# One chain for the RMS norm and the query layer norm, its scale folded into Wq, in a gated cross-attention kernel on Trainium2

## What is computed

```python
# layer 0
memory_proj = ctx @ W_mem.T
attn = softmax(x @ memory_proj.T / sqrt(256))
memory_context = attn @ memory_proj
gate = sigmoid(concat([x, memory_context]) @ W_gate.T + b_gate)
fused = x + gate * memory_context
x = fused * rsqrt(mean(fused ** 2) + 1e-6) * norm_w
# layer 1, 16 heads of 64
qn = (x - mean(x)) * rsqrt(var(x) + 1e-5) * ln_q_g + ln_q_b
q = qn @ Wq * 64 ** -0.5
k, v = split(ctx @ Wkv)
attn = softmax(where(mask, q @ k.T, lowest))
x = x + tanh(attn_gate) * ((attn @ v) @ Wo)
h = layernorm(x) * ln_ff_g + ln_ff_b
x = x + tanh(ff_gate) * (gelu(h @ W1) @ W2)
```

## Time and profile before

| | |
|---|---|
| median of 3 runs | 231.49 us (231.4 to 231.99) |
| profiled execution, its own time | 232.58 us |
| its span | 230.7 us |
| busy share PE, DVE, ACT, POOL | 92%, 61%, 55%, 34% |
| mean granted TensorE clock | 0.993 |

### The profile page before, as it was taken

How to read it: one execution, slowest core, us unless ns; L and a number is a source line. 1 busy time by engine, 2 the same in 40 slices (tenths; PEclk the granted TensorE clock), 3 DMA queues, 4 the chain that set the end, 5 groups by cost and what they waited for, 6 DMA issues and landing times.

```text
span 230.7 us, 4263 instructions
## 1 busy us (share of the span) xinstructions
PE 212.7 (92%) x1520; PEld 170.0 (74%) x1520; DVE 141.8 (61%) x296; ACT 127.4 (55%) x414; POOL 79.5 (34%) x82
## 2 busy tenths in 40 slices
PE   7769997998999999999999977999989999999994
PEld 4546544766976978976989855778867788998993
DVE  1575997635885556985655887867875567125410
ACT  3365754747457646567636466575449775028600
POOL 2030143943175333266331447636373007000000
PEclk9999997999999999999999999999999999999999
DMA  6984005050000000000000000050000000110011
GB/s 203 351 300 149 0 0 182 3 185 0 0 3 0 3 1 1 3 1 0 3 0 4 0 0 0 3 182 0 3 1 3 1 0 4 47 45 0 4 47 53
DMA packets 8463, 10.30 MB, mean 45 GB/s; under 512 B 754, under 2 KB 7668, under 8 KB 8052
## 3 DMA queue, kind: packets, MB, share of 16 engines
q1 hardware_dynamic: 7908, 9.71, 12.3%
q10 hardware_dynamic: 528, 0.26, 0.4%
HBM read 8.92 MB, written 1.05 MB: 43 GB/s over the span
## 4 chain that ended last, share of the span: by engine, by line
PE 56%; issue 13%; DVE 11%; POOL 10%; ACT 9%; POOLq 0%; ACTq 0%; DVEq 0%
PE bank L379 33%; ACT expd L585 6%; POOL probs L481 5%; PE bank L1080 4%; PE bank L1171 4%; PE bank L1050 3%; PE bank L1027 3%; PE bank L1090 3%; DVE neg_max L784 2%; PE bank L1229 2%; POOL wo_pair L519 1%; DVE probsT L797 1%; PE bank L1116 1%; PE bank L1134 1%; PE bank L1126 1%
## 5 line engine op out<-in xcount | busy, mean ns | idle before, releaser
L585 ACT ACTIVATE expd<-bank,neg_max 128x128 f32<-128x128 f32 (+1 forms) x136 | 50.5, 396 | 38.1 <-DVE neg_max L784 38.0
L481 POOL TENSOR_TENSOR probs<-expd,row_rcp 128x512 f32<-128x512 f32 x40 | 42.3, 1069 | 69.8 <-DVE row_rcp L792 63.2
L784 DVE TENSOR_REDUCE neg_max<-bank 128x4 f32<-128x512 f32 (+1 forms) x40 | 25.7, 683 | 6.0 <-PE bank L1050 3.6
L585 ACT ACTIVATION_READ_ACCUMULATOR expd<-bank,neg_max 128x1 f32 x136 | 29.3, 216 | 0.0
L379 PE MATMUL bank<-xhT_pair,wq_pair 128*128 128x256 f32 x192 | 27.5, 293 | 1.1 <-DVE fused L806 1.1
L379 PEld LDWEIGHTS bank<-xhT_pair,wq_pair 128*128 128x128 f32 x192 | 24.6, 194 | 5.0 <-DVE fused L806 1.9
L379 PE MATMUL bank<-wo_pair,oT_pair 128*128 128x256 f32 x192 | 26.6, 288 | 0.0
L1080 PE MATMUL bank<-ident,probs 128*128 128x128 f32 x160 | 22.6, 277 | 3.7 <-POOL probs L481 3.5
L379 PEld LDWEIGHTS bank<-wo_pair,oT_pair 128*128 128x128 f32 x192 | 23.6, 189 | 1.8
L1080 PEld LDWEIGHTS bank<-ident,probs 128*128 128x128 f32 x160 | 17.7, 140 | 8.4 <-POOL probs L481 7.1
L379 PE MATMUL bank<-wq_pair,gelu_pair 128*128 128x256 f32 x192 | 23.2, 281 | 0.4 <-issue 0.3
(11 more groups left out here) (125 smaller groups left out, 346.9 us busy)
## 6 DMA issues: line engine op xcount, KB each, us to landing
stage<-in_L_xattn_W_dram SPq DMA_DIRECT2D x2, 1024.0 KB, 5.0
x_sb<-in_x_dram SPq DMA_DIRECT2D x4, 256.0 KB, 8.7
wkv_sb<-in_L_xattn_Wkv_dram SPq DMA_DIRECT2D x1, 1024.0 KB, 9.2
stage<-in_L_xattn_Wq_dram SPq DMA_DIRECT2D x1, 1024.0 KB, 10.3
stage<-in_L_xattn_Wo_dram SPq DMA_DIRECT2D x1, 1024.0 KB, 5.4
...
```

Source lines behind the costliest of these rows:

```text
L481: nc.gpsimd.tensor_tensor(probs[:, r, :].rearrange("p (h k) -> p h k", h=hb), expd[:, r, :].rearrange("p (h k) -> p h k", h=hb), row_rcp[: ...
L585: last = nc.scalar.activation(expd[:, r, h * w:(h + 1) * w], SC[n % 2][:, h * w:(h + 1) * w], ACT.Exp, bias=neg_max[:, r, h:h + 1], accum_ ...
L784: nc.vector.tensor_reduce(neg_max[:, r, 0:hb], SC[n % 2][:, :].rearrange("p (h k) -> p h k", h=hb), AX_X, ALU.max, negate=True).then_inc(d ...
```

## The change

The two norms become one chain. DVE no longer waits for the root mean square: it multiplies `fused` by `norm_w` alone, takes the statistics of that product, and works out both quantities whose roots are needed (`squares`); POOL takes the four roots at once. `xhat` scales by the second root, since the RMS factor cancels in a layer norm, apart from the epsilon, which is corrected. POOL multiplies `x_sb` by the first root afterwards, for the residual. The stages `x1` and `ln1` are gone; `rms` now does on DVE what they did, in the place of `rms`.

`ln_q_g` is folded into Wq as a scale per partition, and `ln_q_b` into a bias `q_bias`, which 16 matmuls with one moving column make in the prologue (`qbias`) and which DVE adds where it copied `q` before. So POOL's two passes over `xhat` are gone, and `xhT` waits for DVE.

Key banks are copied out whole, the odd ones by ACT and the even ones by DVE. The prologue is put in another order. The loads of `ln_q_g` and `ln_q_b` are 128x2 elements now and stand right behind Wq.

```diff
-    ("k", "hot", 0), ("splitq", 0), ("k", "hot", 3), ("gate", 0), ("k", "hot", 1), ("fuse", 0), ("rms", 0),
-    ("k", "hot", 2), ("k", "hot", 4), ("xT", 1), ("x1", 0), ("ln1", 0), ("k", "hot", 6), ("xhat", 0), ("k", "hot", 5),
-    ("y", 1), ("splitq", 1), ("k", "hot", 7), ("scores", "ctx", 1, 0), ("v", "hot", 0, 0), ("flag",), ("tiles",),
-    ("v", "hot", 1, 0), ("xhT", 0), ("v", "hot", 0, 1), ("norm", "ctx", 1, 0), ("exp", "ctx", 1, 0), ("q", 0, 0),
-    ("splito", 0), ("splito", 1), ("v", "hot", 1, 1),
+    ("k", "hot", 0), ("splitq", 0), ("k", "hot", 1), ("gate", 0), ("qbias",), ("k", "hot", 2), ("fuse", 0), ("rms", 0),
+    ("splitq", 1), ("k", "hot", 3), ("k", "hot", 4), ("xT", 1), ("xhat", 0), ("k", "hot", 5), ("tiles",),
+    ("y", 1), ("k", "hot", 6), ("xhT", 0), ("flag",), ("k", "hot", 7), ("scores", "ctx", 1, 0), ("q", 0, 0),
+    ("v", "hot", 0, 0), ("exp", "ctx", 1, 0), ("v", "hot", 0, 1), ("norm", "ctx", 1, 0),
+    ("splito", 0), ("splito", 1), ("v", "hot", 1, 0), ("v", "hot", 1, 1),
...
-    ((("x1", 1),), (("ln1", 1), ("q", 0, 3), ("xT", 2)), (("xhat", 1),)),
+    ((("xhat", 1),), (("q", 0, 3), ("xT", 2)), ()),
...
+                            gp.wait_ge(pool["x1"], c - 1)
+                        nc.gpsimd.tensor_tensor(roots[:, :, :].rearrange("p a t -> p (a t)"),
+                                                squares[:, :, :].rearrange("p a t -> p (a t)"), half_pow[:, :], ALU.pow
                                                 ).then_inc(pool["rstd"], 1)
...
+                        rows = x_sb[:, st[1] * T:(st[1] + 1) * T, :]
+                        gp.wait_ge(dve["xhat"], c)
+                        gp.wait_ge(pool["rstd"], c)
+                        nc.gpsimd.tensor_tensor(
+                            rows, rows, rms_r.rearrange("p (t a) -> p t a", a=1).to_broadcast([P, T, D]),
+                            ALU.mult).then_inc(pool["x1"], 1)
...
                     elif kind == "rms":
-                        ve_.wait_ge(act["square"], c)
-                        nc.vector.tensor_scalar(ms[:, :], sumsq[:, :], 1.0 / D, RMS_EPS, ALU.mult, ALU.add
-                                                ).then_inc(dve["ms"], 1)
-                    elif kind == "x1":
 
                         b = st[1]
-                        ve_.wait_ge(pool["rms"], c)
                         if c == 1:
                             ve_.wait_ge(w_in["normw"], 16)
+                        ve_.wait_ge(dve["gated"], T * c)
                         for t in range(T):
-                            last = nc.vector.scalar_tensor_tensor(
-                                x_sb[:, b * T + t, :], fused[:, t, :], rms_r[:, t:t + 1], normw_sb[:, :],
-                                ALU.mult, ALU.mult)
+                            last = nc.vector.tensor_tensor(x_sb[:, b * T + t, :], fused[:, t, :], normw_sb[:, :],
+                                                           ALU.mult)
                         chain(last)
                         tile_stats(b)
-                    elif kind == "ln1":
                         aggregate(mean_var, 0)
-                        nc.vector.tensor_scalar(ve[:, :], mean_var[:, :, 1], LN_EPS, None, ALU.add
-                                                ).then_inc(dve["ve"], 1)
+                        ve_.wait_ge(act["square"], c)
+                        if c > 1:
+                            ve_.wait_ge(pool["rstd"], c - 1)
+                        chain(nc.vector.tensor_scalar(ms, sumsq[:, :], 1.0 / D, RMS_EPS, ALU.mult, ALU.add))
+                        nc.vector.scalar_tensor_tensor(ve, ms, LN_EPS, mean_var[:, :, 1], ALU.mult, ALU.add
+                                                       ).then_inc(dve["ve"], 1)
...
+                        for pair in range(PAIRS):
+                            for k in range(K):
+                                last = nc.tensor.matmul(
+                                    path.bank(st)[:, pair:pair + 1], stage[:, k * INNER + pair * P:k * INNER + (pair + 1) * P],
+                                    lnq_cols[:, 1, k:k + 1], start=k == 0, stop=k == K - 1)
+                        last.then_inc(pe["qbias"], 1)
                     elif kind in ("xhT", "h2T"):
-                        te.wait_ge(pool["affine"], c if kind == "xhT" else B + c)
+                        if kind == "xhT":
+                            te.wait_ge(dve["xhat"], c)
```

More of the change, by code:

```diff
@@ L221, in gated_attention_block @@
         sumsq = sb("sumsq", [P, T])
-        ms = sb("ms", [P, T])
-        rms_r = sb("rms_r", [P, T])
-        ve = sb("ve", [P, T])
-        rstd = sb("rstd", [P, T])
+        squares = sb("squares", [P, 2, T])
+        ms, ve = squares[:, 0, :], squares[:, 1, :]
+        roots = sb("roots", [P, 2, T])
+        rms_r, rstd = roots[:, 0, :], roots[:, 1, :]
         ve2 = sb("ve2", [P, B, T])
@@ L280, in gated_attention_block @@
         out_done = sem("out_done")
-        pe = {k: sem(f"pe_{k}") for k in ("xT", "ctxT", "gatew", "gatem", "mask", "y", "scores", "spread",
+        pe = {k: sem(f"pe_{k}") for k in ("xT", "ctxT", "gatew", "gatem", "mask", "qbias", "y", "scores", "spread",
                                           "u", "gate", "xhT", "k", "v", "q", "av", "wo", "h2T", "ff1", "ff2")}
@@ L286, in gated_attention_block @@
         dve = {k: sem(f"dve_{k}") for k in ("xT", "u", "ctxT", "gatew", "wmem", "bgate", "negmax", "rcp", "spread",
-                                            "gated", "ms", "ve", "xhat", "xhT", "k", "v", "q", "o", "wo",
+                                            "gated", "lnq", "qbias", "ve", "xhat", "xhT", "k", "v", "q", "o", "wo",
                                             "ve2", "x2hat", "h2T", "gelu", "out", "wsplit", "mask")}
-        pool = {k: sem(f"pool_{k}") for k in ("rms", "rstd", "probs", "rstd2", "wsplit", "scaled", "affine")}
+        pool = {k: sem(f"pool_{k}") for k in ("rstd", "x1", "probs", "rstd2", "wsplit", "scaled", "affine")}
         PRO = list(PROLOGUE)
@@ L314, in __init__ @@
                 for at, st in enumerate(self.plan):
-                    n = {"xT": 1, "ctxT": 1, "weights": 4, "tiles": 1, "y": 1, "u": 1, "gate": 2, "xhT": 1, "k": 1,
+                    n = {"xT": 1, "ctxT": 1, "weights": 4, "tiles": 1, "qbias": 1, "y": 1, "u": 1, "gate": 2, "xhT": 1, "k": 1,
                          "v": 1, "q": 1, "h2T": 1, "ff1": 1, "ff2": 1}.get(st[0], 0)
@@ L429, in _ @@
             load(stage[:, :].rearrange("p (k n) -> p k n", k=K), wq.rearrange("(p k) n -> p k n", k=K), w_in["wq"])
+            for i, v in enumerate((lnq_g, lnq_b)):
+                load(lnq_cols[:, i, :], v.rearrange("(p k) -> p k", k=K), w_in["lnq"])
             load_x(1)
@@ L761, in run @@
                         nc.vector.reduce_max(tile_any[:, :], mask_tiles[:, :], AX_X).then_inc(dve["mask"], 1)
+                        ve_.wait_ge(w_in["lnq"], 32)
+                        nc.vector.tensor_scalar(lnq_cols[:, :, :], lnq_cols[:, :, :], DH ** -0.5, None, ALU.mult
+                                                ).then_inc(dve["lnq"], 1)
+                    elif kind == "qbias":
+                        ve_.wait_ge(pe["qbias"], 1)
+                        nc.vector.tensor_copy(q_bias[:, :], path.bank(st)[:, 0:PAIRS]).then_inc(dve["qbias"], 1)
                     elif kind == "flag":
@@ L858, in run @@
                         ve_.wait_ge(pe["q"], c)
+                        if c == 1:
+                            ve_.wait_ge(dve["qbias"], 1)
                         if b:
```

88 lines of the change are left out of this document (46 added, 42 removed).

## The result

The changed kernel takes **245.73 us** (median of 4 runs, 244.53 to 246.81) against 231.44 (231.21 to 231.99) for the kernel before on the same chip: ratio **1.0612**, 95% interval 1.0544 to 1.0681. The forecast was 242.6, its range 235 to 247. The profiled execution is the one of 244.53 us. In every ratio, runs more than 1.5% above the fastest of their kernel are left out.

A forecast was written before the change was run, and what follows sets the result against it. PE was taken as the bound, busy 92% of the span and holding 56% of the chain. Slot 1's 6.1 plus the prologue's 5.3 less 0.3 gave +11.1 on 231.5, so 242.6 us, range 235 to 247.

The forecast's parts named there:

- Bias passes: Prologue: the 32 PE passes of qbias take 0.109 us each, 3.5 us in all; bounds 1.8 and 6.1.
- Slot 1, batch 0: DVE's 2.35 us norm chain stands ahead of unit 2's query copy: scores +1.7 us, probs +1.8.
- Batch 1: Slot 1: norm chain delays unit 2's query copy, and ln2 then precedes the maxima; transposes come +2.25 us.
- Batch 2: Slot 1: no query copy in the way, but 2.2 us stand ahead of the maxima; +2.05 us by unit 3.
- Prologue: Step-by-step walk through the prologue: first head exponential at 49.1 against 43.81, +5.3 us.
- 0.86 + 1.72 + 1.42: Prologue: last key matmul, two layer-0 scores and query projection on PE, from 38.9 to 42.9 us.
- POOL: POOL's busy time falls by 2.3 us per batch, to about 70; 0.7 of that for a root.
- PE idle +8: Whole kernel: PE's total idle time must grow by about 8 us, named as the quickest test.
- The sum: Slot 1's 6.1 plus the prologue's 5.3, less 0.3, is +11.1 us, added to the 231.5 median: 242.6; chance 0.55.
- Rival 2: The clock falls once or twice in the new waits, 1.65 us each: about 245 us; chance 0.15.
- Rival 1: Only the prologue loses, as PE time in slots 1 to 3 may hold slack: about 236 us; chance 0.15.
- Rival 3: Faster: prologue saves POOL's passes over xhat if qbias takes under 1.3 us and slot 1 costs nothing: 228.5; chance 0.10.

The follow-up runs named there:

- e4: The kernel before with only the key banks copied whole, odd ones by ACT and even ones by DVE: 231.31 us, ratio 0.9983.
- e12: The kernel before with whole key banks and two value matmuls moved ahead in the prologue, around xhT: 231.41 us, ratio 0.9988.
- e5: The changed kernel with DVE's norm chain cut in two in slot 2, before and behind unit 2's reciprocals: 242.37 us, ratio 1.0414.
- e11: e6 with e9's scalar squares and only 2 of the 32 bias passes: 233.64 us, ratio 1.0108.
- e6: e5 with the prologue nearly in the order of before, the bias passes behind xhT: 241.02 us, ratio 1.0395.
- e9: e5 with DVE's second square written as one scalar operation for each of two columns: 241.9 us, ratio 1.0444.

## Why the prediction was right, and where it was short

The direction, the two places and most terms held. Point by point:

- **Bias passes:** taken at 0.109 us each, the spacing of f32 transposes, and measured at 0.109 (3.49 for 32). The Trainium skill (TensorE: Matmul & The Clock Gate, Back-to-back issue gap) states 81 ns at 128 columns, from which 2.6 us were estimated; this trace disagrees, and the measurement decides.
- **Slot 1, batch 0:** predicted a copy 2.2 us behind `oT_pair` and +1.7 to 1.8. Measured 2.1 us and +1.4. The second part of the term, `probs` later by 1.8, came to nothing: unit 3 was no later than unit 2. **Batch 1:** predicted +2.25, measured +1.65, for the same reason. **Batch 2:** predicted +2.05, measured +2.4: 1.7 at unit 3's scores, and 0.7 behind them. Those 0.7 are what is left of 1.5 us of half clock (scores and output projection last from 149.04 to 153.11, 2.5 us at the full clock) after the places where before itself waited, 0.81 and 1.01 us at 141.75 and 144.37. Together 5.45, and 0.5 in the tail that I did not trace, against 6.1 less 0.3. From the last unit's scores to the end are 59.45 us before and 59.99 in the change, but 58.85 in e4 and 59.54 in e12, so part of that 0.5 may be scatter. That the sum comes so close is partly luck: batches 0 and 1 were put too high by 0.4 and 0.6, batch 2 and the tail too low by 0.35 and 0.5.
- **Prologue:** predicted +5.3, measured +6.0. The walk itself was good to half a microsecond: squares at 30.45 against 30.52, the last key matmul at 38.9 against 38.46. The step that failed is "0.86 + 1.72 + 1.42": from there to the end of the query projection I put 4.0 us, and it took 5.76, because the clock halved.
- **The query copy's new form and the whole key banks** at nothing: the copy with its bias takes 0.69 as before, and e4 measured the banks.
- **POOL** at about 70: measured 71.1. The product took 1.04 as taken, but the four roots take 1.03 where two took 0.70, so a batch saves 0.37 there and not 0.7.
- **PE idle +8:** measured +6.1, since 3.5 of the loss are passes and some 2.4 are half clock, which both count as busy. "The quickest test" was a poor one.
- **The sum.** The traces say +12.0 against +11.1. The medians say +14.3. The remaining 2.3 are a mistake of the last step: I carried the difference over to the median as if both kernels lost the same to the clock. Before's profiled execution lay 1.1 above its median, the changed kernel's lies 1.2 below its own. Of the change's four runs two are at 244.6 with a clock of 0.983 and 0.986, two at 246.8 with 0.972.

Rival 2 (the clock falls in the new waits, about 245, chance 0.15) was given as an alternative to the forecast. It came true on top of it, and its price of 1.65 per fall is what the traces show (1.6 and 1.5). Its 244.3 to 245.9 hold the measured median, which is 3.1 us from the forecast's own number. Rival 1 fell with the waits at unit 2 and with e5: that time had no slack. Rival 3's condition, passes under 1.3 us, was not met; e11, which all but takes the passes away, shows how near the rest is. Its first scores are 1.3 us ahead of before's profile, but about 1.1 of that is before's own fall of the clock, which e11's profile does not have. The part behind them gives 1.07 back, so even then the kernel is 1% slower.

What no run tells: why the clock falls in some runs of one program and not in others, and whether short passes or the DVE waits between them weigh more in that. The bias passes seem to raise the odds (all four runs of e6 were below 0.99, two of e11's at 1.00), but the profiles of the change, e5 and e9 have the passes without a fall behind them, and two runs of e11 fell nearly without passes. They are neither enough nor the only cause.
